# Chunk 0's masked products ahead of a statistics step, and the routing drain in another order

## What is computed

```python
x = x + 0.5 * _L0_ffn_ref(_layernorm(x), ...)    # top-2 of 8 LoRA experts on a shared gated FFN of width 512
x = x + _L0_attn_ref(_layernorm(x), ...)         # gated scan over the tokens, then an MLP of width 384
x = x + 0.5 * _L0_ffn_ref(_layernorm(x), ...)
x = x + 0.5 * _L1_ffn_ref(_layernorm(x), ...)    # top-1 of 8 experts: own layer norm scale, FFN 128-512-128
x = x + _L1_attn_ref(_layernorm(x), ...)         # softmax attention in each sequence of 512
x = x + 0.5 * _L1_ffn_ref(_layernorm(x), ...)
```

## Time and profile before

| what | us |
|---|---|
| median of 3 runs (968.59 to 969.45) | 968.78 |
| the profiled execution | 970.89 |
| its span, first to last instruction | 969.1 |
| end of the last rank on PE (chunk 7, slot 18) | 629.6 |
| end of the last scatter's issue | 637.3 |
| first expert tile on PE | 640.8 |

### The profile page before, as it was taken

The page is one execution under the profiler, slowest core; times in us unless marked ns, Lnnn a source line. Parts: engine busy times, 40 slices in busy tenths (PEclk is TensorE's granted clock), DMA queues, the critical chain, the costliest instruction groups (busy, mean ns, idle before and its releaser), DMA issues. The chain is left out here.

```text
span 969.1 us, 17609 instructions
## 1 busy us (share of the span) xinstructions
PE 919.5 (95%) x5060; PEld 698.9 (72%) x5067; DVE 685.0 (71%) x2098; ACT 555.7 (57%) x1255; POOL 592.3 (61%) x565
## 2 busy tenths in 40 slices
PE   6999999999999999999999999889998999989996
PEld 3777777777777767777767776568994676658996
DVE  5657678888888797888898787474542567665553
ACT  4444655766757577674664443135663676635663
POOL 5678868868577586776867876544441244552443
PEclk8899999999999999999999999999999999999999
DMA  6890000000000000000000000435544000005552
GB/s 182 356 404 2 1 1 1 1 1 1 1 1 1 1 1 1 2 0 1 12 1 12 13 1 27 146 105 179 180 148 119 2 13 23 24 32 152 179 178 87
DMA packets 39774, 62.74 MB, mean 65 GB/s; under 512 B 7073, under 2 KB 23266, under 8 KB 37504
## 3 DMA queue, kind: packets, MB, share of 16 engines
q1 hardware_dynamic: 35136, 53.08, 16.7%
q0 software_dynamic: 4544, 8.54, 2.6%
HBM read 34.68 MB, written 27.82 MB: 64 GB/s over the span
## 5 line engine op out<-in xcount | busy, mean ns | idle before, releaser
L384 PE MATMUL bank<-split 128*128 128x512 f32 x544 | 244.0, 448 | 5.8 <-POOL split L1816 3.0
L386 PE MATMUL bank<-split 128*128 128x512 f32 x544 | 214.9, 395 | 0.0
L385 PE MATMUL bank<-split 128*128 128x512 f32 x544 | 213.8, 393 | 0.0
L909 ACT ACTIVATE sil<-bank 128x512 f32<-128x512 f32 x128 | 76.0, 594 | 147.2 <-PE bank L386 146.7
L384 PEld LDWEIGHTS bank<-split 128*128 128x128 f32 x544 | 103.0, 189 | 36.0 <-issue 10.4
L385 PEld LDWEIGHTS bank<-split 128*128 128x128 f32 x544 | 103.4, 190 | 26.3 <-issue 10.5
L1295 DVE TENSOR_TENSOR act<-bank,sil 128x512 f32<-128x512 f32 x128 | 87.7, 685 | 48.3 <-PE bank L386 25.4
L386 PEld LDWEIGHTS bank<-split 128*128 128x128 f32 x544 | 102.9, 189 | 23.8
L1772 POOL TENSOR_TENSOR act<-act 128x512 f32<-128x512 f32 x64 | 88.6, 1384 | 27.9 <-DVE act L1301 27.7
L1778 POOL TENSOR_TENSOR split<-act,split 128x512 fp32r<-128x512 f32 x64 | 89.7, 1403 | 16.5 <-ACT split L976 16.2
L735 PE MATMUL bank<-xlT,e 128*128 128x128 f32 x624 | 84.2, 278 | 7.8 <-ACT hT_e L1172 4.5
(11 more groups left out here) (314 smaller groups left out, 2010.7 us busy)
## 6 DMA issues: line engine op xcount, KB each, us to landing
e<-e_dram SPq DMA_DIRECT2D x78, 256.0 KB
rows_in<-yw SPq DMA_DIRECT2D x17, 1056.0 KB, 17.9
xin<-rows_in SPq DMA_DIRECT2D x78, 66.0 KB
e<-e_dram SPq DMA_DIRECT2D x4, 512.0 KB, 7.9
x<-rows_out SPq DMA_DIRECT2D x8, 256.0 KB, 4.6
rows_in<-yw,slot_i POOLq DMA_INDIRECT x64, 2.3
rows_out<-ob,ids POOLq DMA_INDIRECT x39
out<-ob,ids POOLq DMA_INDIRECT x39
```

The costliest lines, as they stand in the source:

```text
L384: mm(dst, w[0], m[0], start=start, stop=False, **more)
L385: mm(dst, w[0], m[1], start=False, stop=False, **more)
L386: return mm(dst, w[1], m[0], start=False, stop=stop, **more)
L909: af(sil[(k - 1) % 2][:, :], bank[BH1[STEPS[k - 1][0] % 2]][:, :], ACT.Silu).then_inc(silu_done.sem, 1)
```

## The change

- **Start.** For chunk 0, DVE's `masked(0)` moves from its place behind `f_stats` into it, between `moments` and `aggregate` of chunk 1. The clearing of `zrow` moves from after slot -1 to after slot -2, so SP issues the zero writes sooner.
- **Drain, slots 16 to 18.** PE's `r_rank` moves from behind `fill(4)` to ahead of `r_T`; `r_T` now waits for `rank_read`, and `r_rank` no longer for `xnT_saved`. ACT's `r_alpha` moves ahead of `out_T`. DVE's `r_rows` moves to right behind `r_top1`, so ahead of `r_factors`, `f_add` and `r_stats`. The subtraction r1 = r2 - r1 goes from POOL to DVE, right behind `second_values`. In slot 16 POOL sends blocks 0 to 2 of chunk 5's scatter where `values` stood, ahead of `r_scale(7)`; block 3 keeps the old place.

```diff
 # PE
+                if s.m >= MAINS:
+                    r_rank()
                 r_T()
...
                 fill(4)
-                r_rank()
+                if s.m < MAINS:
+                    r_rank()
 # PE, in r_T
-                        pe.wait_ge(*top1_steps(s.r_sort, 1))
+                        pe.wait_ge(*(rank_read(s.r_sort) if s.m >= MAINS else top1_steps(s.r_sort, 1)))
 # PE, in r_rank
-                    if s.r_pre is not None:
+                    if s.r_pre is not None and s.m < MAINS:
                         pe.wait_ge(*xnT_saved(s.r_pre))
 # ACT
                 silu(4)
+                if s.m >= MAINS:
+                    r_alpha(s.r_sort)
                 out_T()
 # DVE, f_stats
                     moments(xc(n), stats_f, bn_f)
+                    if q == 0:
+                        masked(0)
                     dve.wait_ge(*normed_f(n - 2))
 # DVE, second_values
+                    if s.m >= MAINS:
+                        dve.wait_ge(*r_done(l))
+                        v.tensor_tensor(r1[:, :], r2[:, :], r1[:, :], ALU.subtract).then_inc(r_ready.sem, 1)
 # DVE
                 r_top1(s.r_sort)
+                if s.m >= MAINS:
+                    r_rows(s.r_sort, BSIDE)
                 slot_ratio()
 # POOL
                 values()
+                if s.m == MAINS:
+                    r_scatter(s.r_sort, range(T - 1))
                 a_sum()
...
                 if s.m >= MAINS:
-                    r_scatter(s.r_sort)
+                    r_scatter(s.r_sort, range(T - 1, T) if s.m == MAINS else range(T))
...
-                if s.m == -1:
+                if s.m == -2:
                     pool.memset(zrow, 0.0).then_inc(zeroed.sem, 1)
```

More of the change, by code:

```diff
@@ L1108, in first_layer @@
                 a_mid_T()
-                r_alpha(s.r_sort)
+                if s.m < MAINS:
+                    r_alpha(s.r_sort)
                 r_T(s.r_pre, BSIDE)
@@ L1486, in first_layer @@
                 a_leaky(0)
-                masked(0)
+                if q != 0:
+                    masked(0)
                 act(7)
@@ L1491, in first_layer @@
                 a_leaky(1)
-                r_rows(s.r_sort, BSIDE)
+                if s.m < MAINS:
+                    r_rows(s.r_sort, BSIDE)
                 a_scans()
@@ L1788, in values @@
                 def values():
-                    if l is None:
+                    if l is None or s.m >= MAINS:
                         return
@@ L1910, in r_scale, with r_scatter @@
                 pool.tensor_tensor(nb_r[:, :], sc[:, 3, :], mv_r[n % 2][:, :], ALU.mult).then_inc(rstd_r.sem, 1)
-            def r_scatter(n):
+            def r_scatter(n, blocks=range(T)):
                 if n is None:
@@ L1918, in r_scatter @@
                 pool.wait_ge(*alpha_ready(n))
-                for t in range(T):
+                for t in blocks:
                     pool.indirect_dma_start(rows_in[:, :], bass.IndirectOffsetOnAxis(slot_i[n % 4][:, t:t + 1], 0), yw[n % 4][:, t, :], None
```

## The result

The changed kernel takes 972.82 us (median of 22 runs, 970.26 to 976.26); the kernel before, run beside it, takes 969.6 (22 runs, 968.19 to 973.0). The ratio is 1.0029, with a 95% interval of 1.0019 to 1.0039: slower by 2.8 us, or 3.2 by the medians. I had forecast a shift of +1.1 (968.78 to 969.9) within 968.0 to 971.4. The sign was right, the size was a third of the real one, and the time lies outside the range. The rival of the half clock that lasts through slot 18 had said 972.5.

The account below looks back on a forecast made before the run. PE, busy in 95% of the span, was taken to bound the kernel. Start +0.2, `zrow` clearing 0 and drain +0.9 summed to +1.1, from 968.78 to 969.9 us, range 968.0 to 971.4.

Parts of the forecast that it names:

- The rival of the half clock that lasts through slot 18: Drain, PE: clock stays at half through slot 18, in all +3.7, 972.5; chance 0.13.
- Start: Slot 0's entry: PE's LoRA product +0.87, transposes +0.40, in all +0.2 (bounds 0 to +0.9).
- The `zrow` clearing: POOL at the start: its 1.85 us move to about 7.0, into a wait for ACT; effect 0.
- Tail of item 15: Drain: subtraction on DVE ends at 612.1; `lora_out`, `out_T` and `back` come 0.56 sooner.
- DVE's and POOL's order: Drain: `f_add` behind the waiting `r_rows(5)` +1.3; `r_scale(7)` behind scatter blocks at 620.8; `r_T(7)` +1.2.
- rival 1: Drain: the clock stays up, `r_rank(7)` at 629.0, in all -0.1, 968.7; chance 0.20.
- Fall of the clock: Drain, PE: clock falls at about 624, after 2.7 us with nothing to do ahead of `r_T(7)`.
- Length of the half clock: Drain, PE: `r_T(7)` and six fills at half clock, `r_aff(7)` at 627.7, +1.8; `r_rank(7)` at 630.25, +0.9.
- rival 2: Drain: half clock through slot 18, `r_rank(7)` 3.5 late, in all +3.7, 972.5; chance 0.13.
- The base: Starting point: old drain's rank at 629.33 from one profile, and the median of the runs, 968.78.
- The scatters: Drain, POOL: last scatter starts at 635.9 (636.31 before); PE reaches the first tile at 641.6 without waiting for it.

Follow-up runs that it names:

- start alone: Only the edits of the start, made on the kernel before; ratio to before 1.0004 (0.9989 to 1.0019).
- combined kernel: Changed kernel with the old start, `f_add` ahead of `r_rows`, only block 0 ahead of `r_scale(7)`, 7 fills before `r_T(7)`; 969.51 against 970.65 before, ratio 0.9981.
- the run with 12 fills: Changed kernel plus 12 fills on PE in slot 17, between chunk 6's rank and `r_T(7)`; ratio to before 1.0008 (0.9994 to 1.0021).
- the run with POOL's order changed: Changed kernel with slot 16 in old order, scatter whole, and chunk 0's first `up_low` ahead of chunk 1's `f_scale` on POOL; ratio to before 1.0001.

## Why the prediction was wrong

Point by point, by its steps:

- **Start.** Right: `ud` at 20.73 (said 20.5), `aggregate` ending at 22.31 (22.1), the product at 24.95 (24.85), the transposes at 26.39 (26.3), +0.25 for my +0.2, though this last agreement is that of one pair. The `zrow` clearing fell at 7.21 into POOL's wait, and the zero writes began at 19.94; neither shows on the path.
- **Tail of item 15.** Right: `lora_out` at 612.81, 0.37 sooner in absolute time and 0.62 from `second_values`; the subtraction took 0.69, with a scatter's issue under way on POOL.
- **DVE's and POOL's order.** Right: `f_add` at 617.07 (said 617.0, or 617.2 with the start), statistics ending at 620.33 (620.2), `r_scale(7)` behind the third block at 621.04 (620.8), `r_T(7)` at 624.72 (624.5). The experiments split this: 1.1 for `f_add`'s place, 0.67 for the blocks (I had 0.5 in the step and 0.4 in rival 1).
- **Fall of the clock.** Right in place, just ahead of 624, and in all five profiles. By the rule of the Trainium skill (TensorE: Matmul & The Clock Gate, part on HAM oscillation) it should not have fallen for a gap of 2.77 us; these rows don't agree with it.
- **Length of the half clock.** This is the step that failed: "four fills (1.72) and two more (0.8) run at half clock: `r_aff(7)` at 627.7", and everything from there at full. In the profile of the changed kernel `r_aff(7)` came at 628.19 and itself took 1.72, at half clock. The forecast is one of two outcomes, that of two profiles in five; there the last rank came at +19.6, for which the forecast's 0.9 over the +18.69 of before is right to 0.1. In the other three the half clock went on through `r_aff(7)` and the eight fills, to +22.23. That is rival 2, with its 3.5 for the drain (measured 22.23 - 18.69 = 3.54), to which I gave 0.13. I had argued against it that the fills leave PE no gap. They left none, and the clock stayed at half for over 9 us all the same; the argument had no row behind it beyond one stretch that ended sooner.
- **The base.** I took the +18.69 of one profile for the old order. The start alone showed the same order at +17.78 with the clock at full, so the old order, too, has a shorter outcome, and the changed one is further from it than I reckoned. By the ratios the time went up by 1.8 to 3.5 us in three comparisons that contain the new drain. The median of three runs that I started from, 968.78, also lay 0.8 below the 969.6 of 22 runs: of the 2.9 between 969.9 and 972.82 this is 0.8, and the shift 2.1.
- **The scatters.** They ended later, not sooner (640.03 against 637.27), as chunk 7's blocks wait for the last rank. That PE would start the tiles without waiting for a scatter was right: it took 11.27 from the last rank to the first tile (said 11.35). The work brought forward had room to gain only where the last rank doesn't come later. In the combined kernel it did, by 2.0 us at the first tile.

Five profiles are too few for the odds of the two outcomes. Which one comes goes with where the fall lands in PE's idle time, but what places the fall stays open. How much of the difference of the medians they make up is an inference from these profiles: the clock at the start varies too (in all, 7 to 17 us of the first 31 were at half), so the mean clock of an execution doesn't tell which outcome its drain had. That the half clock in the drain is what costs most there is shown by the rows of the run with 12 fills.

## What to carry over

Work moved ahead of a wait has to be checked for what stands behind it on the same engine: here six tiny instructions of a chunk that had time, and their wait for that chunk's rank, held up the last producer of the chunk that had none, and the three scatter blocks did so again on the next engine. Filler multiplications belong into the gap that a new order opens, not where the old order had it; moving a short step across them moves the gap. And where a half clock lies on the path, its price can be a pair of outcomes and not a number, as here, so the range must reach to the worse one.

## What I had not expected of the hardware

The granted clock stayed at half from 624 to 634 while PE was busy without a gap from 624.72 on; with the same instructions in another execution it was back at about 627.5. And the same gap of 1.33 us was followed by a fall in one execution of the old order and not in another.

DVE instructions of 128 x 4 elements with both inputs in SBUF took 1.23 to 1.25 us, instead of some 0.16, when a POOL instruction of 1.27 to 1.28 us was under way (and 21.67 in the run with POOL's order changed); `ua`, which reads PSUM too, took 0.67 beside the same POOL instruction. The Trainium skill (SBUF — State Buffer, "Who interferes with whom") says that such an instruction contends with a POOL instruction that reads SBUF, and one with at most one SBUF input, outside the 2-port modes, doesn't; the rows agree.
